# Fourteen rows instead of sixteen in each page copy of a paged-attention cache

## What is computed

```
x = x + einsum('bsi,boi->bso', x, weight[adapter_ids])
kc = k_cache[block_table].reshape(bsz, L, HK, D)        # L = 16 pages * 32 keys
vc = v_cache[block_table].reshape(bsz, L, HK, D)
k_all, v_all = concat([kc, k]), concat([vc, v])
scores = where(valid, einsum('bqhd,bkhd->bhqk', q, k_all) * SCALE, -1e30)
x = x + einsum('bse,de->bsd', softmax(scores) @ v_all, Wo)
```

## Time and profile before

| What | Value |
|---|---|
| Runs | 1029.21, 1030.2, 1034.73 us; median 1030.2 |
| Profiled execution | 1032.49 us |
| Its span | 1030.7 us |
| Busy in the span | PE 98%, DVE 83%, ACT 78%, POOL 76% |
| Mean granted TensorE clock | 0.995 |
| Moved by DMA | 179.53 MB in 472125 packets |
| Page copies | 80 on SP's queue, 48 on ACT's, 256 KB each |

### The profile page before, as it was taken

How to read it: one execution, slowest core, us unless ns; L and a number is a source line. 1 busy time by engine, 2 the same in 40 slices (tenths; PEclk the granted TensorE clock), 3 DMA queues, 4 the chain that set the end, 5 groups by cost and what they waited for, 6 DMA issues and landing times.

```text
span 1030.7 us, 19556 instructions
## 1 busy us (share of the span) xinstructions
PE 1006.8 (98%) x5510; PEld 870.7 (84%) x5510; DVE 855.8 (83%) x1779; ACT 801.7 (78%) x2092; POOL 784.1 (76%) x802
## 2 busy tenths in 40 slices
PE   7799899999999999999999999999999999999997
PEld 5587788888888888888888888888888888888885
DVE  6574567666899999989998989998999999998894
ACT  4363556565789888898899888898899888988884
POOL 3786667575498978898798978898798978888662
PEclk9999999999999999999999999999999999999999
DMA  8598989888488979998899888987889879987973
GB/s 271 151 265 282 261 243 220 237 225 219 103 149 173 158 148 164 161 167 149 157 161 162 160 143 171 162 169 151 155 160 171 148 148 165 167 163 139 154 150 64
DMA packets 472125, 179.53 MB, mean 174 GB/s; under 512 B 415042, under 2 KB 452051, under 8 KB 469971
## 3 DMA queue, kind: packets, MB, share of 16 engines
q1 hardware_dynamic: 366384, 148.93, 70.3%
q10 hardware_dynamic: 104610, 27.26, 12.4%
q0 software_dynamic: 1024, 2.10, 0.7%
HBM read 109.25 MB, written 35.66 MB: 141 GB/s over the span
## 4 chain that ended last, share of the span: by engine, by line
PE 87%; SPq 8%; DMA 2%; issue 2%; DVE 1%; ACT 0%; POOL 0%; ACTq 0%; POOLq 0%
PE S L1278 20%; PE O L1211 7%; PE O L1213 7%; PE O L1212 7%; PE Y L1211 5%; PE Q L1213 5%; PE Q L1211 5%; PE Y L1213 5%; PE Y L1212 5%; PE Q L1212 5%; PE T L1217 5%; SPq L299 4%; PE KV L1211 3%; PE KV L1212 3%; PE KV L1213 3%
## 5 line engine op out<-in xcount | busy, mean ns | idle before, releaser
L964 DVE CUSTOM_DVE_ANT_0 pr<-S,mask,rst 128x640 f32<-128x640 f32 x256 | 225.2, 880 | 29.5 <-PE S L1278 25.2
L989 DVE SCALAR_TENSOR_TENSOR pr<-pr,rc,raw 128x640 f16<-128x640 f32 x204 | 239.9, 1176 | 11.8 <-ACT raw L749 5.6
L769 ACT ACTIVATE pr<-pr,nb 128x640 f32<-128x640 f32 x256 | 211.8, 827 | 24.9 <-DVE nb L964 24.8
L749 ACT ACTIVATE raw<-pr,rc 128x640 f16<-128x640 f32 x204 | 163.4, 826 | 3.4 <-DVE rc L980 3.1
L569 POOL TENSOR_TENSOR m<-m 128x512 f32<-128x512 f32 x64 | 111.5, 1743 | 65.2 <-DVE m L1017 62.2
L1278 PE MATMUL S<-kh,qh 128*128 128x320 f32 x512 | 121.0, 317 | 5.5 <-DVE nb L964 5.0
L523 POOL TENSOR_TENSOR kl<-raw,kh 128x512 fp32r<-128x512 f32 x64 | 97.8, 1528 | 33.6 <-ACT kh L658 32.6
L544 POOL TENSOR_SCALAR ptl<-first 128x512 fp32r<-128x512 f16 x130 | 102.1, 785 | 21.8 <-DMA first<-pr 11.7
L1278 PE MATMUL S<-kh,ql 128*128 128x320 f32 x512 | 117.0, 310 | 0.0
L1278 PE MATMUL S<-kl,qh 128*128 128x320 f32 x512 | 116.4, 309 | 0.6 <-POOL kl L523 0.6
L710 ACT ACTIVATE Q<-Q 128x128 f32<-128x128 f32 x256 | 68.3, 267 | 60.1 <-DVE m L1017 60.1
(11 more groups left out here) (137 smaller groups left out, 2705.1 us busy)
## 6 DMA issues: line engine op xcount, KB each, us to landing
cache_rows<-in_kv SPq DMA_DIRECT2D x80, 256.0 KB, 5.2
wraw<-in_wall SPq DMA_DIRECT2D x74, 256.0 KB, 4.4
raw<-cache_rows SPq DMA_DIRECT2D x63, 256.0 KB, 4.1
raw<-cache_rows ACTq DMA_DIRECT2D x49, 256.0 KB, 5.3
cache_rows<-in_kv ACTq DMA_DIRECT2D x48, 256.0 KB, 5.5
mask<-mask_rows SPq DMA_DIRECT2D x64, 128.0 KB, 3.9
first<-in_lw SPq DMA_DIRECT2D x6, 1024.0 KB, 7.8
acc<-in_x SPq DMA_DIRECT2D x8, 256.0 KB, 7.5
```

The lines of the kernel that those rows point to most:

```text
L749: e.activation(upper16[:, g, :], pr[:, slot(u, g), :], ACT.Copy, scale=rc[:, u % 2, g:g + 1]).then_inc(a_f1, 1)
L769: e.activation(pr[:, slot(u, g), :], pr[:, slot(u, g), :], ACT.Exp, bias=nb[:, u % 2, g:g + 1], scale=-1.0, accum_out=sm[:, u % 2, g:g + 1 ...
L964: e.tensor_tensor_reduce(pr[:, slot(u, g), :].rearrange("p (a n) -> p a n", a=2), S[:, :, 0:320], mask[:, u % 2, :].rearrange("p (a n) -> ...
L989: e.scalar_tensor_tensor(out=lower16(u, g), in0=pr[:, slot(u, g), :], scalar=rc[:, u % 2, g:g + 1], in1=upper16[:, g, :], op0=ALU.mult, op ...
```

## The change

The copies leave out rows 0 and 1 of cache_rows, the value and the key row of head 0, at both places where they are issued. Each of the 128 DMAs then has 14 rows of 16 KB, 224 KB, where it had 16 rows. cache_rows keeps its size, and the number of DMAs, their order, their queues and their semaphores stay as they are. Nothing reads rows 0 and 1 of cache_rows, before or after.

```diff
             def copy_pages(b, t):
...
                     e.dma_start(
-                        copy[:, b, 4 * t + j, :],
-                        kv[:, bass.ds(numbers[j], 1), :].rearrange("r a n -> (r a) n")
+                        copy[2:, b, 4 * t + j, :],
+                        kv[2:, bass.ds(numbers[j], 1), :].rearrange("r a n -> (r a) n")
                     ).then_inc(d_copy[b], 16)
...
             def copy_page(b, k, number):
-                e.dma_start(copy[:, b, k, :],
-                            kv[:, bass.ds(number, 1), :].rearrange("r a n -> (r a) n")
+                e.dma_start(copy[2:, b, k, :],
+                            kv[2:, bass.ds(number, 1), :].rearrange("r a n -> (r a) n")
                             ).then_inc(d_copy[b], 16)
```

## The result

| | Runs | Median us | Lowest to highest |
|---|---|---|---|
| Kernel before | 20 | 1031.83 | 1027.69 to 1035.87 |
| Changed kernel | 20 | 1034.70 | 1028.50 to 1039.49 |

The ratio of the changed kernel to the kernel before is 1.0032, with a 95% interval of 1.0018 to 1.0046: 3.3 us slower, 1.9 to 4.7. That is inside the range of the prediction and within the 0.5% that it called no change, but the interval is clear of zero and the sign is not the one of the 0.2 us that the forecast had put on the fast side. An eighth of the copied bytes went, and the kernel lost time. That the time still lies inside the range owes something to luck: the issue cost more than its upper bound, and other effects of the same change hid part of it.

The account below looks back on a forecast made before the run. SP's issuing and a late weight chunk were taken to bound the kernel before about 107 us, a gapless TensorE afterwards. Terms of 0 + 0 + 0 + 0 left the 1030.2 us median; forecast 1030.0 us, range 1026 to 1036.

Parts of the forecast that it names:

- What bounds the kernel: Before about 107 us SP's issuing and a late weight chunk lie on the path; afterwards copies run beside a gapless TensorE.
- Issue on SP's path ... I take 0: Twelve SP copies in the first 97 us issue at an unchanged 0.492 us each: 0, from -0.7 to +1.9 us.
- After 107 us SP and ACT issue under a TensorE that has no gap: 0: Copies issued after 107 us lie beside a TensorE that waits for nothing, so their issue adds 0 us.
- The slowest are among the fourteen, and nothing has been taken from them: On the DMA engines: two are spared, fourteen keep 0.84 us a packet, so no transfer lands sooner.
- the hold-up term: SP held up by full queues issuing key pages, excess 8.2 us on the path: taken as unchanged, -1.0 to 0 us.
- The late chunk: Head 1's first weight chunk, issued at 96.75 us: 0, from -0.8 to 0 us; the whole event costs about 4.9 us.
- The forecast's sign of landings near 5.2 and 5.5 us: Expected in the profile after: a copy's median time to landing still near 5.2 and 5.5 us.
- Rival B: Issue of fourteen rows is dearer, at L392 before 97 us; decides from 0.43 us more per copy, 5.2 us; chance 0.05.
- Rival A: Memory, not the engine, limits the copies: 1027.7 us, or 1023.6 if the late chunk's event vanished; chance 0.12.
- key pages below 15.35 and 13.78 us: Sign for Rival A: issue of the key pages near 50 and 75 us takes less than these times.
- Rival C: Fourteen rows go to seven DMA engines, two packets each, in the first 260 us: 1095 us; chance 0.03.

Follow-up runs that it names:

- e4: Kernel before with fourteen-row copies as in the change, but each row cut into sixteen outer pieces of 1 KB; ratio to before 0.9938, -6.4 us.
- e13: Kernel before with the form of e4 only for the 32 copies before about 107 us, sixteen whole rows later; ratio to before 0.9963, -3.8 us.
- e17: Kernel before plus 40 DMAs of several forms at its end on SP's idle queue; only issue read: memory to memory, fourteen rows 0.76 us, sixteen 0.59.
- e5: The changed kernel, unaltered, measured and profiled a second time; ratio to the kernel before 1.0048, +5.0 us.
- e1: Kernel before with copies leaving out row 0 alone, fifteen rows of 16 KB each; ratio to before 1.0077, +7.9 us.
- e7: Kernel before with fourteen rows only in the 96 later copies, sixteen in the 32 early ones; ratio to before 1.0011, +1.1 us.
- e16: The kernel of e7 measured once more, sixteen rows early and fourteen late; ratio to the kernel before 1.0004, +0.4 us.
- e10: Kernel before, sixteen rows, with four groups of page copies moved from SP to ACT in periods 8 to 11; ratio to before 0.9979, -2.2 us.
- e8: Kernel before, sixteen rows, with a register load added after each copy, though the trace has no row of these loads; ratio to before 1.0003, +0.3 us.
- e6: Kernel before with fourteen rows only in the 32 early copies (sequences 0 and 1), sixteen in the other 96; ratio to before 1.0005, +0.5 us.
- e9: Changed kernel, fourteen rows, with four groups of page copies moved from SP to ACT in periods 8 to 11; ratio to the kernel before 1.0003, +0.3 us.
- e3: Kernel before with copies leaving out the rows of heads 0 to 3, eight rows each, output not the reference's; ratio to before 0.9954, -4.7 us.

## Why the prediction was wrong, point by point

- **What bounds the kernel: right early, incomplete late.** SP's issuing and the late weight chunk set the start, as read from the earlier trace rows; e4 takes 6.9 us off the chunk's issue and 6.4 us off the kernel, but not one for one: e13 takes 7.8 us off the chunk's issue and 3.8 off the kernel.
- **"Issue on SP's path ... I take 0", from -0.7 to +1.9 us: this term failed.** It was measured at 0.774 - 0.492 = 0.28 us a copy, nearly twice the bound of 0.16. Twelve copies make 3.4 us at the medians, 2.7 in the profile. The bound came from the eight-row transfers of the earlier trace rows, 0.36 and 0.34 us; one of them ends in SBUF and the other starts there, and e17 shows that into SBUF a smaller count costs nothing (out of SBUF was not tried). The nearest row was nearest in its count and not in its kind.
- **"After 107 us SP and ACT issue under a TensorE that has no gap: 0": this step failed too.** The cover was real and the pace of units 2 to 10 the same, but a queue has its own limit. Sixty of SP's copies lie in 157 to 262 us. They took 19.8 us more in the changed kernel (60 x 0.28 = 17 by the medians) and the loads of values among them 5.7 more, which used up the 27.9 us in which SP had waited, and what came next in SP's queue, unit 14's keys and the first transposes, was late. In the profiles of e5, e1 and e7 that cost 4.4 to 5.4 us, in the change's first and in e16 0.4 to 0.8. How much of the measured 3.3 and 5.0 us it makes on average is not shown (e7, e16 and the control e10 speak for less than all). The prediction named no work that would be late next there.
- **"The slowest are among the fourteen, and nothing has been taken from them": wrong in its result.** Key pages issued in 25.3 and 25.8 us (changed, e5) where the kernel before took 29.1, so against that one profile the hold-up term, 0 with -1.0 as its end, was about -3.5 us. Other profiles shrink it: with the same early copies as before, e8 took 29.4 and e10 25.4, and with fourteen rows e6 and e9 took 24.8 and 26.7. On the mean of each group the relief is about 2.3 us, with overlap. It offset most of the issue's +2.7 us early. Part of the relief may be the slower issue itself: the share of the DMA engines up to 107 us fell from 0.81 to 0.76 in the changed kernel, and to 0.76 with fifteen rows as well. Whether fourteen rows really lie on fourteen engines no run shows.
- **The late chunk: nearly right.** Issued at 97.37 and rounded at 104.67, 7.3 us after (7.7 in e5) against 8.8 before: -1.1 to -1.5 us, forecast 0 with -0.8 as its end. ACT's wait, expected at 8 to 9 us, was 6.8 and, in e5, 8.5. The forecast's sign of landings near 5.2 and 5.5 us can't be read: the profiles give no time to landing for copies of fourteen rows. Those of fifteen (e1) landed after 4.0 us on SP and 5.7 on ACT.
- **Rival B (dearer issue) had the mechanism right and the place wrong.** It put the place at L392 before 97 us and its point of decision at 0.43 us a copy, for a loss of 5.2 us. At the measured 0.28 its own sum, 12 x 0.28 = 3.4 us, happens to equal the measured 3.3; that is chance, since the profiles show most of it offset before unit 2 and e6 has only +0.5 us. Its sign in the profile, L392 at 0.7 us or more, is what the profile shows. Rival A has some truth in e3 and e4, where fewer bytes seem to help; its sign, key pages below 15.35 and 13.78 us, was seen, but e10 shows it with sixteen rows too. Rival C did not happen.

## What to carry to other kernels

A queue that is not on the critical path still has a budget: add up its idle time in the stretch and compare that with the number of its instructions times the change in each, and look at what stands first behind the stretch. When a transfer is made smaller, look at the shape that is left; fourteen rows cut into sixteen outer pieces took 6.4 us off this kernel, the same bytes in fourteen rows added 3.3 to 5.0. One profile of each kernel is not enough to split a loss of 3 us into places: here two executions of the same instructions differed by more. And a run that adds instructions says something only once the trace shows them. A price taken from a neighbouring row holds only if source, destination and shape are of its kind.

## What was not expected of the hardware

A DMA of this kernel between two places in device memory, at a page number from a register, takes 0.49 us to issue with sixteen outer rows, and 0.81, 0.77, 0.74 and 0.63 us with fifteen, fourteen, twelve and eight; into SBUF the same reduction makes the issue cheaper (0.42, 0.38 and 0.30 us for sixteen, fourteen and eight partitions, e17).
